# Query and key products term by term, and the token banks filled by transposes, in a fused block of channel attention, token attention and experts

## The chip, the cores and the metric

The kernel runs on one core of a Trainium2 chip. The metric is the device time of one execution in microseconds, median of several. A core has TensorE (PE, matrix products; its weight loads are shown apart as PEld), VectorE (DVE), ScalarE (ACT), GpSimd (POOL) and SyncE (SP, which here only issues DMA). Each takes its own instructions in order and waits on semaphores for the others.

## The reference

```python
# layer 0, per image (16 images, 192 channels, 32 x 32 points)
xn = (x - mu) * rsqrt(var + EPS) * ln_g + ln_b
Q, K, V = (dwconv3x3(per_head_1x1(xn)) for each of q, k, v)       # 8 heads of 24
attn = softmax(einsum('bhnc,bhnd->bhcd', K, Q) / alpha)           # channels x channels
x = einsum('bcij,oc->boij', V attn, w_f) + b_f + xn
# layer 1, on tokens t [16, 1024, 192]
t = t + causal_attention(_ln_t(t))        # 6 heads of 32, output projected twice
t = t + experts(_ln_t(t))                 # 4 experts of 768, top 2, gelu
```

All is float32; the gates choose the experts from the normed tokens.

## The kernel before

A first part runs over the 16 images, one after the other; a second runs over 67 blocks of 512 routed rows and does the experts. Only the first part is touched. Each engine has one program, written out by hand in order; nothing reorders it but the weight loads of PE. In an image of 1024 tokens in 8 chunks of 128:

1. The convolutions give query, key and value channels; channel attention is computed and folded with w_f into mixing matrices `mix`.
2. **Token banks.** For each chunk k one PSUM bank (`token_bank(k)` = k modulo 6) collects the tokens of the chunk, 192 columns of channels and 4 of gates: `input_and_first_heads` brings in the normed image `xn` (two halves of 96 channels, as products with an identity), the gate columns, and the first heads; `last_heads` the others. DVE takes each bank (`channel_mixed`, line 1045, signal `y_sb`), takes statistics (`first_stats`), and POOL raises the variance to the power -1/2 (`token_rstd`, line 716).
3. **Norm.** DVE writes the normed chunks (`normed`, line 1021), four at a time, PE transposes them (`norm_transposes`, line 1714) into two banks. ACT copies these rounded (`T0`, `T1`; line 1458, signal `T_hi`), DVE forms the remainders (`low_channels`, lines 1029 and 1032; `T2` and the lower part of `T1`; signal `T_lo`).
4. **Query and key products** (`queries_keys`, line 1731). There are six groups n, each a weight block f for a half nh of the tokens, in the order of `QK_ORDER`; each is five products of 512 columns (the entries of `qkv`: two with T0, one with T2, two with T1) into bank n modulo 4. ACT copies the group (`QKh`, line 1551), DVE forms its remainder (`low_qk`, line 1038, signal `qk_lo`). Groups 0 to 2 and the values of two chunks come ahead of the norm transposes of the second half, groups 3 to 5 behind them.
5. **Values** (`values_of_tokens`, line 1739): five products of 192 columns for each chunk.
6. SP and POOL copy QKh and QKl into stacks `KS`, `QS` by DMA, in three waves of tokens; from them come the scores (line 1770), exponentials, block transposes (line 1782) and the weighted values of the causal attention. POOL copies the inverse sums wide (`inverse_wide`, lines 728 and 729) for PE's transposes at line 1822.

DVE's order in steps 2 to 4 matters: chunks 0 to 4, `normed` of the first half, chunks 5 and 6, `low_channels` of the first half, chunk 7, `low_qk(0)`, `normed` of the second half, `low_qk(1)` and `(2)`, `low_channels` of the second half, `low_qk(3)` to `(5)`. Between these steps stands part of the previous image's routing; its rows are scattered by POOL (`send`, line 780, two scatters for each chunk).

The waits of `queries_keys`: a group n below 4 waits for `y_sb`, since its bank was a token bank: n = 0 for chunk 6's bank, n = 1 and above for chunk 7's; n = 4 and 5 wait for `low_qk` of groups 0 and 1.

Of the kernel before, what the change touches and what calls it, by code (L numbers as in the profile page):

```python
# [15 lines left out]
P = 128  # L16
# [3 lines left out]
def hybrid_block_kernel(nc, x, ln_g, ln_b, conv_w, conv_bias_row, conv_taps, conv_bias, alpha_rows, w_f_t, b_f,  # L20
                        w_qkv_a, w_qkv_b, w_proj, w_proj_t, b_proj, gate_w_a, gate_w_b, gate_b, w1_a, w1_b, b1_t,
                        w2, b2, out):
    B, C, SH, SW = x.shape
    N = SH * SW
    NC = N // P
    HALF = C // 2
# [13 lines left out]
    E = gate_w_a.shape[1]  # L40
# [3 lines left out]
    CE = C + E  # L44
    QC = N // BANK
    TPC = BANK // P
# [24 lines left out]
    with ExitStack() as ctx:  # L71
# [183 lines left out]
        def bank(b, n=1):  # L255
            return ps[:, b * BANK:(b + n) * BANK]
# [200 lines left out]
        NORM_BANK = (6, 4)  # L457

        def value_bank(k):
            return (6, 7, 4, 5)[k % 4]  # L460

        QK_ORDER = [(0, 0), (1, 0), (2, 0), (0, 1), (1, 1), (2, 1)]
        NQ = len(QK_ORDER)
# [186 lines left out]
        def _(pool):  # L650
# [138 lines left out]
            for i in range(B):  # L789
                unpad_image(pool, i)  # L790
                if i:
                    send(i - 1, 0, 3)
                token_rstd(i, 0)
                if i:
                    send(i - 1, 3, 5)
                token_rstd(i, 1)
                if i:
                    send(i - 1, 5, 6)
                pool.wait_ge(qk_hi, NQ * i + PAIR_GROUPS)
                for j in range(2):  # L800
                    load_queries(g, 0, j, 0, QKh)
                    load_queries(g, 0, j, 2, QKh)
                pool.wait_ge(qk_lo, NQ * i + PAIR_GROUPS)
                for j in range(2):
                    load_queries(g, 0, j, 1, QKl)
                if i:
                    send(i - 1, 6, NC)
                output_bias(i, 0)
                for qc in range(NC):
                    inverse_wide(i, qc)  # L810
                    if qc == 0:
                        output_bias(i, 1)
                    if qc == 2 and i + 1 < B:
                        image_rstd(pool, i + 1)
                    if qc == TPC:
                        token_rstd2(i, 0)
                    if i + 1 == B:
                        split_behind(qc)
                token_rstd2(i, 1)
# [603 lines left out]
        def _(act):  # L1423
# [31 lines left out]
            def high_channels(i, j):  # L1455
                for n, dst in enumerate((T0, T1)):
                    act.wait_ge(lnT_ps, 4 * i + 2 * j + n + 1)
                    a.activation(dst[:, BANK * j:BANK * (j + 1)], bank(NORM_BANK[j] + n), ACT.Copy).then_inc(T_hi, 1)
# [67 lines left out]
            for i in range(B):  # L1526
                conv_qk(i, 0)
                if i:
                    gate_exp(i - 1)
                conv_out(i, 2)  # L1530
                conv_qk(i, 1)
                conv_out(i, 3)
                channel_exp(i, 0)
                conv_out(i, 4)
                conv_qk(i, 2)
                mixing(i, 0)
                conv_out(i, 5)
                conv_qk(i, 3)
                channel_exp(i, 1)
                mixing(i, 1)  # L1540
                high_channels(i, 0)
                for n in range(NQ):
                    if n == QK_FIRST:
                        for k in range(2):
                            values_out(i, k)
                        high_channels(i, 1)
                    f, nh = QK_ORDER[n]
                    if i == 0 and n == 0:
                        act.wait_ge(w_ld["zero"], 16)
                    act.wait_ge(qk_ps, NQ * i + n + 1)  # L1550
                    a.activation(QKh[:, f, BANK * nh:BANK * (nh + 1)], bank(n % 4), ACT.Copy).then_inc(qk_hi, 1)
                for k in range(2, NC):
                    values_out(i, k)
                for n, (qc, h) in enumerate(SOFT):
                    exponentials(i, n)
                    if n:
                        blocks_out(i, n - 1)
                    if qc and h == 2:
                        norms_out(i, qc - 1)
                blocks_out(i, NU - 1)  # L1560
                if i + 1 < B:
                    for r in range(2):
                        conv_out(i + 1, r)
                norms_out(i, NC - 1)
# [44 lines left out]
        def _(pe):  # L1609
# [82 lines left out]
            def input_and_first_heads(i, k):  # L1692

                o = bank(token_bank(k))
                t.matmul(o[:, 0:HALF], xn[:, 0, P * k:P * (k + 1)], ident[0:HALF, 0:HALF],
                         start=True, stop=False, skip_group_check=True)
                t.matmul(o[:, C:CE], xn[:, 0, P * k:P * (k + 1)], gcol[:, :], start=False, stop=False,
                         skip_group_check=True)
                t.matmul(o[:, HALF:CE], xn[:, 1, P * k:P * (k + 1)], ident_g[:, :], start=False, stop=False,
                         skip_group_check=True)  # L1700
                t.matmul(o[:, 0:CE], vp[:, 0, P * k:P * (k + 1)], mix[:, 0, :], start=False, stop=False,
                         skip_group_check=True)

# [13 lines left out]

            qkv = ((T0, wqa_hi), (T0, wqa_lo), (T2, wqa_hi), (T1, wqb_hi), (T1, wqb_lo))

            def queries_keys(i, n):  # L1720
                f, nh = QK_ORDER[n]
                if n >= 4:
                    pe.wait_ge(qk_lo, NQ * i + n - 3)
                if n < 4:
                    pe.wait_ge(y_sb, NC * i + min(NC - 1 + n, NC))
                for m, (act_part, w_part) in enumerate(qkv):
                    if f == 0 and m in (0, 3):
                        pe.wait_ge(T_hi, 4 * i + 2 * nh + 1 + m // 3)
                    if f == 0 and m in (2, 3):
                        pe.wait_ge(T_lo, 4 * i + 2 * nh + m - 1)  # L1730
                    last = t.matmul(bank(n % 4), w_part[:, P * f:P * (f + 1)],
                                    act_part[:, BANK * nh:BANK * (nh + 1)], start=m == 0, stop=m == 4)
                last.then_inc(qk_ps, 1)

            def values_of_tokens(i, k):
                if k >= 4:
                    pe.wait_ge(v_done, NC * i + k - 3)
                for m, (act_part, w_part) in enumerate(qkv):
                    last = t.matmul(bank(value_bank(k))[:, 0:C], act_part[:, P * k:P * (k + 1)],
                                    w_part[:, 2 * C:3 * C], start=m == 0, stop=m == 4)  # L1740
                last.then_inc(v_ps, 1)
# [105 lines left out]
            for i in range(B):  # L1847
# [32 lines left out]
                    input_and_first_heads(i, k)  # L1880
                    last_heads(i, k)
                norm_transposes(i, 0)
                for n in range(QK_FIRST):
                    queries_keys(i, n)
                for k in range(2):
                    values_of_tokens(i, k)
                norm_transposes(i, 1)
                for n in range(QK_FIRST, NQ):
                    queries_keys(i, n)
                for k in range(2, NC):  # L1890
                    values_of_tokens(i, k)
                if not i:
                    pe.wait_ge(setup_pool, 8)
# [179 lines left out]
```

## Time and profile before

| | |
|---|---|
| median of 3 runs (lowest, highest) | 3336.41 us (3331.54, 3340.59) |
| profiled execution, its own time | 3334.18 us |
| its span in the trace | 3332.3 us |
| PE busy | 3067.4 us, 92% |
| DVE busy | 2202.3 us, 66% |
| ACT busy | 1871.5 us, 56% |
| POOL busy | 874.5 us, 26% |

The images take the time to about 2210 us, the experts the rest. Times in the trace are from the start of the span; all numbers below are in that clock. A row of the timeline has start, duration, engine, line, operation and the idle time ahead of it with what ended it. Durations of products overlap, so the cost of one in a row is the distance of the starts.

### The profile page before, as it was taken

To read this page: it belongs to the slowest core of one execution; us is meant where nothing else is said; L and a number is where in the kernel's file an instruction comes from. 1 tells how busy PE (TensorE), PEld (TensorE's weight loads), DVE (VectorE), ACT (ScalarE), POOL (GpSimd) and SP (SyncE) were. 2 spreads that over 40 slices of the span, in tenths; PEclk is the share of its full clock that TensorE was granted. 3 is DMA by queue.
4 is the path that set the end of the run, shared out by engine and by line. 5 is a ranking of instruction groups with operands and counts; after the bars stand their busy time and mean duration, and the time that the engine had idled before them with its cause. 6 is when DMAs were issued, how large, how long until landed. Compare 5 with 4: busy or idle time off the path is not lost. (4 is left out here: it accounts for less than half of the span.)

```text
span 3332.3 us, 72396 instructions
## 1 busy us (share of the span) xinstructions
PE 3067.4 (92%) x26642; PEld 2344.2 (70%) x26642; DVE 2202.3 (66%) x5619; ACT 1871.5 (56%) x3996; POOL 874.5 (26%) x1142
## 2 busy tenths in 40 slices
PE   4999999999999999999999999958999999999995
PEld 1666667666666676666766766637888888888884
DVE  3777677677776776777767767664555655655653
ACT  0647456465474664654746647535555555555553
POOL 2121313303223133132230331450223223223222
PEclk9999999999999999999999999979999999999997
DMA  7546445454364454544644546515667767667673
GB/s 177 142 114 178 115 124 148 124 150 126 113 184 116 122 149 122 153 118 120 173 125 115 148 123 154 156 47 159 195 206 213 221 208 220 210 205 228 206 212 120
DMA packets 256516, 519.82 MB, mean 156 GB/s; under 512 B 70919, under 2 KB 161991, under 8 KB 246521
## 3 DMA queue, kind: packets, MB, share of 16 engines
q1 hardware_dynamic: 222878, 453.58, 48.6%
q0 software_dynamic: 29184, 59.81, 6.0%
q8 instruction: 217, 3.56, 0.4%
q10 hardware_dynamic: 4107, 1.81, 0.3%
q14 instruction: 130, 1.06, 0.1%
HBM read 242.82 MB, written 117.71 MB: 108 GB/s over the span
## 5 line engine op out<-in xcount | busy, mean ns | idle before, releaser
L1051 DVE TENSOR_REDUCE minus_max<-ps 128x1 f32<-128x128 f32 (+7 forms) x768 | 571.6, 750 | 243.7 <-PE ps L1772 232.3
L1469 ACT ACTIVATE p_sb<-ps,minus_max 128x128 f32<-128x128 f32 (+7 forms) x768 | 569.3, 741 | 41.3 <-DVE minus_max L1051 37.8
L1782 PE MATMUL ps<-ident,p_sb 128*128 128x128 f32 x3456 | 530.6, 279 | 44.2 <-ACT p_sb L1469 18.4
L1356 DVE TENSOR_TENSOR g_lo<-g,g_hi 128x512 fp32r<-128x512 f32 x402 | 282.8, 704 | 369.3 <-ACT g_hi L1593 369.3
L1592 ACT ACTIVATE g<-ps,bcur 128x512 f32<-128x512 f32 x402 | 276.6, 688 | 429.2 <-PE ps L1967 429.2
L1483 ACT ACTIVATE PT<-ps 128x512 f32<-128x512 f32 (+3 forms) x768 | 396.7, 517 | 132.7 <-PE ps L1782 123.5
L1782 PEld LDWEIGHTS ps<-ident,p_sb 128*128 128x128 f32 x3456 | 370.0, 141 | 99.4 <-ACT p_sb L1469 37.5
L1983 PE MATMUL ps<-w_all,g_hi 128*128 x1608 | 434.6, 351 | 0.0
L1770 PE MATMUL ps<-KS,QS 96*128 96x512 f32 (+3 forms) x1152 | 393.6, 401 | 21.4 <-ACT p_sb L1469 17.9
L1647 PE MATMUL ps<-ring,wconv 125*32 125x512 f32 (+1 forms) x3072 | 358.4, 606 | 15.0 <-DMA ring<-padded_scratch 15.0
L780 POOL DMA_INDIRECT routed_rows<-xhat,slot x256 | 253.3, 989 | 358.2 <-issue 358.2
L846 POOL DMA_INDIRECT got<-expert_rows,slot x256 | 257.6, 1006 | 333.6 <-issue 270.7
L728 POOL COPY inverse_wide<-inverse_sums 128x192 f32<-128x192 f32 x128 | 44.2, 345 | 1040.3 <-DVE inverse_sums L1072 1040.3
L1988 PE MATMUL ps<-w_all,g_lo 128*128 x1608 | 293.1, 264 | 0.0
L1988 PEld LDWEIGHTS ps<-w_all,g_lo 128*128 128x128 f32 x1608 | 289.4, 188 | 2.0
L1983 PEld LDWEIGHTS ps<-w_all,g_hi 128*128 128x128 f32 x1608 | 263.8, 191 | 22.8
L1593 ACT ACTIVATE g_hi<-ps,bcur 128x512 fp32r<-128x512 f32 x402 | 273.5, 680 | 0.0
L1967 PE MATMUL ps<-X_hi,cur 128*128 128x512 f32 x804 | 264.9, 411 | 7.5 <-ACT g_hi L1593 5.6
L1967 PE MATMUL ps<-X,cur 128*128 128x512 f32 x804 | 250.0, 392 | 0.0
L1770 PEld LDWEIGHTS ps<-KS,QS 96*128 96x128 f32 x1152 | 196.9, 195 | 69.4 <-ACT p_sb L1469 42.4
L1647 PEld LDWEIGHTS ps<-ring,wconv 125*32 125x32 f32 (+1 forms) x3072 | 94.2, 111 | 207.5 <-issue 192.7
L1064 DVE COPY PT<-ps 128x128 f32<-128x128 f32 (+3 forms) x384 | 184.9, 482 | 67.6 <-PE ps L1782 67.5
(276 smaller groups left out, 5442.5 us busy)
## 6 DMA issues: line engine op xcount, KB each, us to landing
ring<-padded_scratch SPq DMA_DIRECT2D x576, 204.0 KB
cur<-w_all SPq DMA_DIRECT2D x67, 1536.0 KB, 7.1
routed_rows<-zero_rows SPq DMA_DIRECT2D x67, 384.0 KB, 5.0
xgt<-routed_rows SPq DMA_DIRECT2D x67, 384.0 KB, 4.6
expert_rows<-y_rows SPq DMA_DIRECT2D x67, 384.0 KB, 3.0
padded_scratch<-xpad SPq DMA_DIRECT2D x32, 435.0 KB, 3.6
x_sb<-x SPq DMA_DIRECT2D x16, 768.0 KB, 5.5
KS<-QKh SPq DMA_DIRECT2D x128, 96.0 KB
```

The source lines that it names most:

```text
L1051: v.tensor_reduce(nmx[:, qc, h:h + 1], score_place(n), AX, ALU.max, negate=True).then_inc(mx_sb, 1)
L1356: v.tensor_tensor(g_lo[:, n % 2, :], g32[:, n % 2, :], g_hi[:, n % 2, :].bitcast(F32), ALU.subtract).then_inc(lo_sb, 1)
L1469: a.activation(p_sb[n % NP][:, 0:P * (qc + 1)], score_place(n), ACT.Exp, bias=nmx[:, qc, h:h + 1], accum_out=ls[:, qc, h:h + 1]).then_inc( ...
L1483: a.activation(PT[h][:, k0:k0 + nb, :], bank(pass_bank(t))[:, 0:P * nb].rearrange("p (k q) -> p k q", q=P), ACT.Copy).then_inc(PT_act, 1)
L1592: a.activation(g32[:, n % 2, :], bank(n % 2), ACT.Gelu, bias=b1)
L1593: a.activation(g_hi[:, n % 2, :], bank(n % 2), ACT.Gelu, bias=b1).then_inc(gelu_sb, 1)
L1647: last = t.matmul(bank(2 * (r % 2) + nh)[W * j:W * (j + 1), :], wconv[s][0:KROWS[s], h, c0:c0 + W], rhs, start=s == 0, stop=s == 1, skip_g ...
L1770: t.matmul(o[:, k0:k0 + keys], QS[0:96, qc // TPC, h, P * (qc % TPC):P * (qc % TPC + 1)], KS[0:96, h, k0:k0 + keys], start=True, stop=k0 + ...
L1782: last = t.transpose(bank(pass_bank(piece))[:, P * k:P * (k + 1)], p_sb[n % NP][:, P * (k0 + k):P * (k0 + k + 1)], ident[:, :])
L1967: last = t.matmul(bank(n % 2), w[:, W1L * part + P * j:W1L * part + P * (j + 1)], act_part[:, :], start=m == 0, stop=m == 4)
L1983: t.matmul(bank(acc_bank(r, tt))[:, 0:2 * C], g_hi[:, n % 2, P * tt:P * (tt + 1)], w2j, start=j == 0, stop=False, skip_group_check=True)
L1988: last = t.matmul(bank(acc_bank(r, tt))[:, 0:C], g_lo[:, n % 2, P * tt:P * (tt + 1)], w2j[:, 0:C], start=False, stop=j == J - 1, skip_grou ...
```

## The change

It has four parts. In the token banks each half of `xn` enters as a transpose (a product in the transposing mode) of 96 columns instead of a product with the identity, and the gate columns of each half come in a product of four columns of their own. In `queries_keys` the three groups of a half are taken together, term by term: the two products with T0 of all three groups, then T2 of all three, then T1 of all three. The values of chunks 2 and 3 move ahead of the second three groups, on PE and on ACT, with other banks. POOL's scatters of chunk 5 move behind its query loads.

```diff
         def value_bank(k):
-            return (6, 7, 4, 5)[k % 4]
+            return (6, 7, 6, 7, 4, 5, 6, 7)[k]
...
                 token_rstd(i, 1)
-                if i:
-                    send(i - 1, 5, 6)
                 pool.wait_ge(qk_hi, NQ * i + PAIR_GROUPS)
...
                 if i:
-                    send(i - 1, 6, NC)
+                    send(i - 1, 5, NC)
...
                         high_channels(i, 1)
+                        for k in range(2, TPC):
+                            values_out(i, k)
...
-                t.matmul(o[:, 0:HALF], xn[:, 0, P * k:P * (k + 1)], ident[0:HALF, 0:HALF],
-                         start=True, stop=False, skip_group_check=True)
-                t.matmul(o[:, C:CE], xn[:, 0, P * k:P * (k + 1)], gcol[:, :], start=False, stop=False,
-                         skip_group_check=True)
-                t.matmul(o[:, HALF:CE], xn[:, 1, P * k:P * (k + 1)], ident_g[:, :], start=False, stop=False,
-                         skip_group_check=True)
+                for h in range(2):
+                    t.matmul(o[:, HALF * h:HALF * (h + 1)], xn[:, h, P * k:P * (k + 1)], ident[0:HALF, 0:HALF],
+                             start=h == 0, stop=False, is_transpose=True, skip_group_check=True)
+                    t.matmul(o[:, C:CE], xn[:, h, P * k:P * (k + 1)],
+                             (gcol[:, :], ident_g[:, HALF:HALF + E])[h], start=False, stop=False, skip_group_check=True)
...
+            def queries_keys(i, nh):
+                group = range(QK_FIRST * nh, QK_FIRST * (nh + 1))
+
+                def term(n, m):
+                    f = QK_ORDER[n][0]
+                    act_part, w_part = qkv[m]
+                    return t.matmul(bank(n % 4), w_part[:, P * f:P * (f + 1)],
                                     act_part[:, BANK * nh:BANK * (nh + 1)], start=m == 0, stop=m == 4)
+                pe.wait_ge(T_hi, 4 * i + 2 * nh + 1)
+                for n in group:
+                    if n >= 4:
+                        pe.wait_ge(qk_lo, NQ * i + n - 3)
+                    else:
+                        pe.wait_ge(y_sb, NC * i + min(NC - 1 + n, NC))
+                    term(n, 0)
+                    term(n, 1)
+                pe.wait_ge(T_lo, 4 * i + 2 * nh + 1)
+                for n in group:
+                    term(n, 2)
+                pe.wait_ge(T_hi, 4 * i + 2 * nh + 2)
+                pe.wait_ge(T_lo, 4 * i + 2 * nh + 2)
+                for n in group:
+                    term(n, 3)
+                    term(n, 4).then_inc(qk_ps, 1)
 
             def values_of_tokens(i, k):
-                if k >= 4:
+                if k in (2, 3):
+                    pe.wait_ge(v_done, NC * i + k - 1)
+                if k in (6, 7):
                     pe.wait_ge(v_done, NC * i + k - 3)
...
-                for n in range(QK_FIRST):
-                    queries_keys(i, n)
+                queries_keys(i, 0)
                 for k in range(2):
                     values_of_tokens(i, k)
                 norm_transposes(i, 1)
-                for n in range(QK_FIRST, NQ):
-                    queries_keys(i, n)
-                for k in range(2, NC):
+                for k in range(2, TPC):
+                    values_of_tokens(i, k)
+                queries_keys(i, 1)
+                for k in range(TPC, NC):
                     values_of_tokens(i, k)
```

On PE, one chunk of the token banks before and after, behind the channel products of line 1674 (line 1695 is the identity product, 1696 in the new kernel the transpose):

```order
L1674 MATMUL ps<-qkt 64x64 x16
L1695 MATMUL ps<-ident,xn 128x96
L1697 MATMUL ps<-gate_cols,xn 128x4
L1699 MATMUL ps<-ident_gate,xn 128x100
L1701 MATMUL ps<-mix,vp 128x196
```

```order
L1674 MATMUL ps<-qkt 64x64 x16
L1696 MATMUL ps<-ident,xn 128x96
L1698 MATMUL ps<-gate_cols,xn 128x4
L1696 MATMUL ps<-ident,xn 128x96
L1698 MATMUL ps<-ident_gate,xn 128x4
L1700 MATMUL ps<-mix,vp 128x196
```

The product of 100 columns is split into a transpose of 96 and a product of 4.

On PE, the first half's groups, behind the norm transposes of image 0; before, the first two groups (T_hi is T0, T_lo is T2, T_128 is T1):

```order
L1731 MATMUL ps<-T_hi,wqkv_a_lo 128x512
L1731 MATMUL ps<-T_lo,wqkv_a_hi 128x512
L1731 MATMUL ps<-T_128,wqkv_b_hi 128x512
L1731 MATMUL ps<-T_128,wqkv_b_lo 128x512
L1731 MATMUL ps<-T_hi,wqkv_a_hi 128x512
L1731 MATMUL ps<-T_hi,wqkv_a_lo 128x512
L1731 MATMUL ps<-T_lo,wqkv_a_hi 128x512
```

```order
L1725 MATMUL ps<-T_hi,wqkv_a_hi 128x512
L1725 MATMUL ps<-T_hi,wqkv_a_lo 128x512
L1725 MATMUL ps<-T_hi,wqkv_a_hi 128x512
L1725 MATMUL ps<-T_hi,wqkv_a_lo 128x512
L1725 MATMUL ps<-T_hi,wqkv_a_hi 128x512
L1725 MATMUL ps<-T_hi,wqkv_a_lo 128x512
L1725 MATMUL ps<-T_lo,wqkv_a_hi 128x512 x3
L1725 MATMUL ps<-T_128,wqkv_b_hi 128x512
L1725 MATMUL ps<-T_128,wqkv_b_lo 128x512
```

Six products now stand ahead of the first that reads the remainder T_lo, and the first group is finished by the eleventh of fifteen instead of by the fifth.

On POOL, between the two roots of the variances and the first wide copy of the inverse sums, before and after (each DMA of line 780 is a scatter of rows, line 357 loads queries):

```order
L716 TENSOR_TENSOR rstd<-rstd,minus_half 128x4
L780 DMA routed_rows<-xhat_0_137,slot 34304x192 x2
L357 DMA QS<-QKh 32x3x256 x4
L357 DMA QS<-QKl 32x3x256 x2
L780 DMA routed_rows<-xhat_0_137,slot 34304x192 x4
L786 TENSOR_TENSOR t_sb<-t_sb,bproj_bc 128x784
```

```order
L716 TENSOR_TENSOR rstd<-rstd,minus_half 128x4
L357 DMA QS<-QKh 32x3x256 x4
L357 DMA QS<-QKl 32x3x256 x2
L780 DMA routed_rows<-xhat_0_137,slot 34304x192 x6
L786 TENSOR_TENSOR t_sb<-t_sb,bproj_bc 128x784
```

Two scatters have moved behind the query loads, so six stand in a row ahead of the bias addition at line 786.

## Rows read from the trace of the kernel before

**Rows 1.** The list of waits of PE: engine line waited for: us, times, longest

```profile
PE ps L1822 <- POOL inverse_wide L729: 14.4, 32, 3.3
```

**Rows 2.** Timeline of PE, eighth image, one chunk of the token banks

```profile
1038.37 0.36 PE L1695 MATMUL ps<-ident,xn 96*128 96x96 f32 x2
1038.56 0.31 PE L1697 MATMUL ps<-gate_cols,xn 96*128 96x4 f32 x2
1038.73 0.45 PE L1699 MATMUL ps<-ident_gate,xn 96*128 96x100 f32 x2
1039.01 0.52 PE L1701 MATMUL ps<-mix,vp 128*128 128x196 f32 x2
1039.37 0.83 PE L1705 MATMUL ps<-mix,vp 128*128 128x196 f32 x4
```

**Rows 3.** Weight loads: line 1695 (ns least/median/most), line 1782 (count, us busy, mean ns)

```profile
L1695 PEld LDWEIGHTS ps<-ident,xn x256: 186/191/193, 90.5 to 2111.7; 96*128 96x128 f32 x128
...
L1782 PEld LDWEIGHTS ps<-ident,p_sb 128*128 128x128 f32 x3456 | 370.0, 141 | 99.4 <-ACT p_sb L1469 37.5
```

**Rows 4.** Timeline of DVE, eighth image

```profile
1037.67 0.63 DVE L1045 TENSOR_TENSOR t_sb<-ps,bf_bc 128x196 f32<-128x196 f32 x2 [0.22 <-PE ps L1705]
...
1046.70 0.36 DVE L1045 TENSOR_TENSOR t_sb<-ps,bf_bc 128x196 f32<-128x196 f32 x1
...
1048.18 0.69 DVE L1038 TENSOR_TENSOR QKl<-ps,QKh 128x512 fp32r<-128x512 f32 x1 [0.30 <-ACT QKh L1551]
1049.04 1.35 DVE L1021 TENSOR_SCALAR xhat<-t_sb,tmv,rstd 128x192 f32<-128x192 f32 x4 [0.17 <-POOL rstd L716]
```

**Rows 5.** Timeline of PE, second image (first row), then the eighth

```profile
247.06 0.44 PE L1714 MATMUL ps<-ident,xhat 128*128 128x128 f32 x2 [0.17 <-DVE xhat L1021]
...
1043.49 1.09 PE L1714 MATMUL ps<-ident,xhat 128*128 128x128 f32 x8 [0.62 <-DVE xhat L1021]
1044.92 0.47 PE L1731 MATMUL ps<-T_hi,wqkv_a_hi 128*128 128x512 f32 x1 [0.34 <-DVE t_sb L1045]
...
1046.81 0.47 PE L1731 MATMUL ps<-T,wqkv_b_hi 128*128 128x512 f32 x1 [0.32 <-DVE T L1032]
1047.12 0.40 PE L1731 MATMUL ps<-T,wqkv_b_lo 128*128 128x512 f32 x1
...
1049.65 0.25 PE L1739 MATMUL ps<-wqkv_a_hi,T_hi 128*128 128x192 f32 x1
...
1050.75 1.04 PE L1714 MATMUL ps<-ident,xhat 128*128 128x128 f32 x8
...
1059.75 0.24 PE L1770 MATMUL ps<-KS,QS 96*128 96x128 f32 x1
```

**Rows 6.** Timeline of ACT, eighth image

```profile
1047.55 0.60 ACT L1551 ACTIVATE QKh<-ps 128x512 fp32r<-128x512 f32 x1 [2.29 <-PE ps L1731]
```

**Rows 7.** Timeline of POOL, sixth image (first row), then the eighth

```profile
791.34 0.96 POOL L780 DMA_INDIRECT routed_rows<-xhat,slot  x1 [1.50 <-issue]
...
1055.25 1.03 POOL L780 DMA_INDIRECT routed_rows<-xhat,slot  x1 [0.30 <-issue]
...
1060.13 1.86 POOL L786 TENSOR_TENSOR t_sb<-t_sb,bproj_bc 128x784 f32<-128x784 f32 x1
1065.24 0.34 POOL L728 COPY inverse_wide<-inverse_sums 128x192 f32<-128x192 f32 x1 [3.25 <-DVE inverse_sums L1072]
```

**Rows 8.** Stretches of 2 us: length, busy PE, PEld, DVE, ACT, POOL, clock, DMA

```profile
104.00:106.00 2.00, 0.58 (x5) 0.58 (x6) 1.81 (x7) 0.00 (x0) 0.01 (x1) 1.00 0.00 0
...
108.00:110.00 2.00, 1.98 (x4) 1.31 (x5) 1.71 (x6) 0.00 (x0) 0.11 (x1) 0.50 0.00 0
...
1044.00:1046.00 2.00, 1.28 (x9) 0.64 (x7) 1.90 (x8) 1.09 (x2) 1.39 (x3) 1.00 0.15 51
```

**Rows 9.** Timeline of PE, first image, query and key products

```profile
109.31 0.63 PE L1731 MATMUL ps<-T,wqkv_b_lo 128*128 128x512 f32 x1
109.74 0.63 PE L1731 MATMUL ps<-T_hi,wqkv_a_hi 128*128 128x512 f32 x1
```

More of the change, by code:

```diff
@@ L1718, in _ @@
             qkv = ((T0, wqa_hi), (T0, wqa_lo), (T2, wqa_hi), (T1, wqb_hi), (T1, wqb_lo))
[L1720 to L1731, printed above, removed]
-                                    act_part[:, BANK * nh:BANK * (nh + 1)], start=m == 0, stop=m == 4)
-                last.then_inc(qk_ps, 1)
+            def queries_keys(i, nh):
[4 more added lines that the diff above has]
+                    return t.matmul(bank(n % 4), w_part[:, P * f:P * (f + 1)],
+                                    act_part[:, BANK * nh:BANK * (nh + 1)], start=m == 0, stop=m == 4)
+                pe.wait_ge(T_hi, 4 * i + 2 * nh + 1)
[14 more added lines that the diff above has]
+                    term(n, 4).then_inc(qk_ps, 1)
             def values_of_tokens(i, k):
-                if k >= 4:
+                if k in (2, 3):
+                    pe.wait_ge(v_done, NC * i + k - 1)
+                if k in (6, 7):
                     pe.wait_ge(v_done, NC * i + k - 3)
@@ L1887, in _ @@
                 norm_transposes(i, 1)
-                for n in range(QK_FIRST, NQ):
-                    queries_keys(i, n)
-                for k in range(2, NC):
+                for k in range(2, TPC):
+                    values_of_tokens(i, k)
+                queries_keys(i, 1)
+                for k in range(TPC, NC):
                     values_of_tokens(i, k)
```

## The prediction

> **What bounds the kernel now.** I read the page first. TensorE (PE) is the busiest engine and the chain that ended last runs mostly over it, so its idle time counts, and only that. The list of waits says where PE idles and for whom; one entry on which a term rests is 14.4 us at the transposes of the inverse sums, for POOL's inverse_wide [rows 1], spread over all images. Then I read one image closely, the eighth, in the timelines of PE, DVE, ACT and POOL from 1029.9 us on. Images 2 to 15 (counted from 0) repeat it within 0.1 us. Image 1 differs in one place, named below. Image 0 has no routing beside it and I give it nothing.
>
> In this image the row to look at is the DVE's. It waits 0.22 us for PE at the first channel_mixed, and from there to the last T_lo remainder it waits for PE nowhere [rows 4]. It computes four normed chunks, on which PE's transposes wait 0.62 us, then chunks 5 and 6, then two remainders (low_channels), and only then channel_mixed of chunk 7, from 1046.70 to 1047.06 [rows 4, 5]. That order is not touched by the change.
>
> **Token banks, part by part.** A chunk takes 0.19 + 0.17 + 0.28 + 0.36 = 1.00 us on PE before the next group starts [rows 2]. Each float32 product is two instructions (the 128 chunks of line 1695 have 256 records), a transpose is one (the blocks of line 1782 have 3456). So a chunk has eight instructions before, and eight after: transpose, 2, transpose, 2, 2 of the mixing. The count does not fall; what may fall is the price of one. The products of four columns cost 0.17 / 2 = 0.085 us each by their starts, and the 96 columns about 0.1 each, so it is the loading of weights and not the streaming that sets them. A transpose's load takes 141 ns where a product's takes 191 [rows 3], 0.05 less. Of the two new transposes one follows a mixing product, under whose streaming its load is hidden before and after; the other can give 0.05 us. Bounds: 0 if loads are paced by something else, 0.11 (a whole pass of 96 columns) above. I take 0.05, by the difference of the load rows.
>
> Who profits? Five chunks stand ahead of the first last_heads, so y_ps comes 0.25 us earlier. DVE could use 0.22 us of it, plus 0.05 because its channel logits, which PE feeds behind chunk 0, come earlier too. So DVE moves ahead by 0.25 us; all other savings of PE (3 more chunks) only lengthen its wait for xhat from 0.62 to about 0.77 us. 0.25 us x 14 images + 0.05 for image 1, where DVE is busy without a gap, is **-3.6 us** (bounds 0 and -4.9).
>
> **Query and key products.** The reordering puts six products (two terms of three groups) ahead of the wait for T_lo. But the second group of a half writes bank 1, which channel_mixed of chunk 7 must have read, and so waits for y_sb 8. DVE gives that after both remainders. So PE does two products (the first at 1044.92, the second 0.31 us later) and stops; the wait for T_lo is not covered but replaced by a longer one. Before, PE went on without a gap from 1046.81 [rows 5]. It started 0.11 us after DVE had gone on to its next instruction (1046.70). After the change the releasing row is that next one, of 0.36 us; with the same lag PE starts at 1046.70 + 0.36 + 0.04 + 0.11 = 1047.2, with 13 products left. By the rows the first spacing is 0.31 us and the rest (1049.65 - 1047.12) / 11 = 0.23 [rows 5]: the values of tokens start at 1047.2 + 0.31 + 12 x 0.227, about 1050.2, where they started at 1049.65. **+0.6 us.**
>
> More follows behind it. Group 0 is now finished by the ninth of these 13, not by the second after the wait. The ninth starts at 1049.1; ACT copies 0.43 us later (before: 1047.12 to 1047.55 [rows 5, 6]), and DVE's low_qk(0), which started 0.63 us after ACT [rows 4], runs from 1050.17 to 1050.86. Behind low_qk(0) in DVE's queue stand the four normed chunks of the second half. They started at 1049.04; now at 1050.85, and end at 1052.2. PE's second set of transposes waits for them: 1052.25 instead of 1050.75 [rows 5], with 0.9 us idle ahead. **+1.5 us there.** In image 1 POOL's late rstd held them back anyway (247.06 is 21.14 us after that image's first product at 225.92, against 20.85 in the eighth [rows 5]), so there it is +1.2.
>
> Then the gain. From the second transposes to the first score PE took 1059.75 - 1050.75 = 9.0 us [rows 5]. It holds 0.92 us of transposes, 15 products x 0.227 = 3.41 and 30 of the values x 0.111 = 3.34, together 7.6; the other 1.4 us are waits for T_hi, T_lo and T. With the values of chunks 2 and 3 (1.1 us) between, ACT and DVE finish T of the second half (about 1055.0) before its first use at about 1055.7, six products into the group. All 1.4 us go. Net at the first score: 1.5 - 1.4 = +0.1 us in 14 images and about -0.3 in image 1, in sum **+1.1 us** (bounds -2 and +5: 0.2 and 0.3 us an image for the lags). What is late next? low_qk of the last group: PE's last three groups now end 0.45 us apart, ACT and DVE need 0.6 to 0.69 each, and DVE ends at about 1059.4; the scores wait for it and start at 1059.85. It is just hidden, by the four chunks of values that are left (2.2 us). It would cost up to 0.5 us an image if the lags are longer.
>
> **POOL.** Two scatters of rows move behind the query loads. The queries are no longer late; nothing waited for that. The other end of the queue: six scatters, 1.28 us apart, from 1055.25 end at 1062.9 instead of 1060.1, the bias addition (1.86 us) ends at 1064.8, and inverse_wide is asked for at 1065.24 [rows 7]. Hidden by 0.4 us. But in 6 of 15 images one of these scatters waits 1.2 to 1.7 us more (1.50 at 791.34 [rows 7]). There inverse_wide comes 0.7 to 1.2 us late and PE, which has almost no slack at the norm transposes, stands. ACT's exponentials are the tight resource in these first chunks, so I count half: 6 x 0.9 / 2 = **+2.7 us** (bounds 0 and 15 x 0.9 = 13).
>
> **The clock.** In image 0 PE's granted clock fell to 0.50 just when it started these products: it had been busy 0.58 of 2 us shortly before [rows 8]. Products are then 0.43 us apart (109.31 to 109.74 [rows 9]) instead of 0.23. In the other images PE was busy 1.28 of 2 us and the clock stayed at 1.00 [rows 8]. The change makes this stretch emptier: between about 1045.6 and 1047.2 PE now does nothing, so 2 us that held 1.3 us of work hold 0.3 to 0.5. A fall costs (0.43 - 0.23) x 8 products ahead of the end of group 0 = 1.6 us at the second transposes, and as much at the scores. No row says how often it will happen. I count 3 falls of 15, nearer to none, because 15 images with 1.28 busy never fell and one with 0.58 did: **+4.5 us** (bounds 0 and 15 x 1.5 = 22).
>
> **Sum.** -3.6 + 1.1 + 2.7 + 4.5 = +4.7 us on the profiled execution's 3334.18, which is 2.2 us under the median of 3336.41. That gives 3338.9 for such an execution and 3341.1 for the median; I predict **3341 us**.
>
> **Rivals.** *The clock falls in most images.* For it speaks that the new idle stretch, 1.7 us behind only two products, is emptier than the one of image 0; against it that the 0.62 us ahead of the transposes and 0.34 us behind them, with two more waits close by [rows 5], never made it fall in 15 images. It would give 15 x 1.5 = 22 instead of 4.5: about 3359. It decides from some eight falls on. The Trainium skill, page "TensorE: Matmul & The Clock Gate", section "Part 4: PE-mode transpose", says that transposes do not count as busy for the clock as products do; by it the eight norm transposes and the new transposes in the banks are no help, and this rival is likelier. The trace agrees in part: in image 0 nearly all that PE did in the emptier stretch was transposes. Chance 0.15.
>
> *POOL becomes late in all images*, since six scatters now run while SP's key and query loads fill the DMA engines: 13 us instead of 2.7, about 3351. For it: extra waits appear only in that stretch. Against it: nine images had none. Chance 0.12.
>
> *The wait is covered as the order intends*: if y_sb 8 were there before T_lo, the second transposes would start no later than now, and the 1.4 us of waits in the second half would go for nothing: 1.5 x 14 = 21 less than in the forecast, about 3320. DVE's order speaks against it. Chance 0.05.
>
> *Forecast*, with parts as above: 0.68.
>
> **How the numbers follow.** A measurement can tell about 0.3% here, 10 us. The forecast's chance splits 0.02 faster, 0.52 within, 0.14 slower (when its two positive terms come out at twice their size); the first rival is slower; the second 0.10 slower and 0.02 within; the third faster. Faster 0.07, same 0.54, slower 0.39. The range reaches from 3330 (both positive terms zero, the bank term in full: 3336.4 - 4.9 - 2 = 3329.5) to 3359, where the first rival lies; beyond are the third rival and the worst of both slow ones.
>
> **What would show it.** Right: in a middle image PE idles about 1.5 us at its third product of the first half with DVE's t_sb as releaser, about 0.9 us at the second transposes behind DVE's xhat, and nowhere in the second half; DVE's wait at the first channel_mixed is gone; bank products have the same count of records. Wrong: idle time still at T_lo or T, the first score more than 0.3 us from 29.8 us after the image's first product without a fall of the clock, a chunk under 0.89 us, or L728 waiting for POOL's own queue in most images.

## The result, and the profile after

The changed kernel takes 3357.11 us (median of 6 runs, 3352.58 to 3360.75); before took 3336.36 us in its 6 runs beside it. The ratio is 1.0063 (95% interval 1.005 to 1.0076): 0.63% slower, about 21 us. The forecast was 3341 with a range of 3330 to 3359; the time lies inside the range, near its upper end.

The profiled execution took 3356.89 us. First its page (span, busy time of each engine, the scatters' line), then the list of waits of PE (us in total, times, longest):

```profile
span 3355.0 us, 72396 instructions
...
PE 3067.1 (91%) x26642; PEld 2350.3 (70%) x26642; DVE 2193.9 (65%) x5619; ACT 1864.6 (56%) x3996; POOL 877.2 (26%) x1142
...
L780 POOL DMA_INDIRECT routed_rows<-xhat,slot x256 | 251.7, 983 | 402.8 <-issue 402.8
```

```profile
PE ps L1713 <- DVE xhat L1019: 35.3, 31, 2.6
...
PE ps L1725 <- DVE t_sb L1043: 22.5, 26, 1.5
...
PE ps L1834 <- POOL inverse_wide L729: 15.5, 31, 4.5
```

PE has as many instructions as before and is busy as long (3067.1 us against 3067.4), so on balance the 22.7 us that the span gained are idle time. The balance hides two changes of the busy time: it is 7.7 us less in the token banks, and 6.1 us more between the first norm transposes and the first score, where products ran at a lower clock (below). Line 1834, where I had put POOL's cost, grew from 14.4 [rows 1] to 15.5 us only. The waits grew at the norm transposes (line 1713, before 10.9 us) and at the query/key products for t_sb (line 1725, before 5.5 us); those for T and T_lo (before 9.8 and 5.6 us) are no longer in the list.

Then one image, the third (number 2, counted from 0), whose first bank product is at 363.7 us. PE:

```profile
377.04 1.09 PE L1713 MATMUL ps<-ident,xhat 128*128 128x128 f32 x8 [0.86 <-DVE xhat L1019]
378.52 0.47 PE L1725 MATMUL ps<-T_hi,wqkv_a_hi 128*128 128x512 f32 x1 [0.39 <-DVE t_sb L1043]
...
380.67 0.50 PE L1725 MATMUL ps<-T_hi,wqkv_a_hi 128*128 128x512 f32 x1 [1.45 <-DVE t_sb L1043]
...
385.57 1.09 PE L1713 MATMUL ps<-ident,xhat 128*128 128x128 f32 x8 [0.57 <-DVE xhat L1019]
...
393.25 0.25 PE L1782 MATMUL ps<-KS,QS 96*128 96x128 f32 x1
```

DVE in the same image:

```profile
371.24 0.63 DVE L1043 TENSOR_TENSOR t_sb<-ps,bf_bc 128x196 f32<-128x196 f32 x2
...
378.81 0.69 DVE L1027 TENSOR_TENSOR T_lo<-ps,T_hi 128x512 fp32r<-128x512 f32 x1
379.53 0.69 DVE L1030 TENSOR_TENSOR T<-ps,T 64x512 fp32r<-64x512 f32 x1
380.25 0.36 DVE L1043 TENSOR_TENSOR t_sb<-ps,bf_bc 128x196 f32<-128x196 f32 x1
...
384.28 1.24 DVE L1019 TENSOR_SCALAR xhat<-t_sb,tmv,rstd 128x192 f32<-128x192 f32 x4
```

This is the picture that the prediction drew. DVE starts `channel_mixed` without a gap (before 0.22 us [rows 4]). PE stands 1.45 us at its third product until both remainders and chunk 7's bank are done, waits again at the second transposes, and reaches the first score 29.6 us after the image's first product. But of all images only this one and the last look quite so. In images 4, 5, 10, 12 and 14 the first transposes come 0.3 to 0.4 us later and the rest is the same. In the seven others from number 3 on they come 1.0 to 1.7 us later. The eighth (number 7, first product at 1036.1) shows what these seven have. POOL first:

```profile
1036.52 1.07 POOL L780 DMA_INDIRECT routed_rows<-xhat,slot  x1 [15.85 <-issue]
1041.73 0.96 POOL L780 DMA_INDIRECT routed_rows<-xhat,slot  x1 [4.14 <-issue]
...
1047.78 1.04 POOL L716 TENSOR_TENSOR rstd<-rstd,minus_half 128x4 f32<-128x4 f32 x1
...
1053.29 0.96 POOL L780 DMA_INDIRECT routed_rows<-xhat,slot  x1 [1.95 <-issue]
```

The same place in the kernel before:

```profile
1032.81 0.96 POOL L780 DMA_INDIRECT routed_rows<-xhat,slot  x1 [0.30 <-issue]
1035.72 0.96 POOL L780 DMA_INDIRECT routed_rows<-xhat,slot  x1 [1.95 <-issue]
...
1038.25 0.96 POOL L780 DMA_INDIRECT routed_rows<-xhat,slot  x1 [0.30 <-issue]
1040.80 1.04 POOL L716 TENSOR_TENSOR rstd<-rstd,minus_half 128x4 f32<-128x4 f32 x1 [1.59 <-DVE rstd L1012]
```

POOL sends six scatters ahead of the first `token_rstd`. Before, the fourth of them stalls for 1.95 us (up to 2.8 in other images), and here POOL still waits 1.59 us for DVE ahead of the rstd. After the change the second one stalls, for 4.14 us; the six end one behind the other, and the rstd comes at once behind the last, 11.7 us after the image's first product instead of 10.9. Then PE in the changed kernel, and two stretches of 2 us of the ninth image (length, busy PE, PEld, DVE, ACT, POOL, clock, DMA):

```profile
1050.47 1.63 PE L1713 MATMUL ps<-ident,xhat 128*128 128x128 f32 x8 [1.83 <-DVE xhat L1019]
1051.95 0.78 PE L1725 MATMUL ps<-T_hi,wqkv_a_hi 128*128 128x512 f32 x1
1052.52 0.63 PE L1725 MATMUL ps<-T_hi,wqkv_a_lo 128*128 128x512 f32 x1
1054.10 0.79 PE L1725 MATMUL ps<-T_hi,wqkv_a_hi 128*128 128x512 f32 x1 [0.95 <-DVE t_sb L1043]
```

```profile
1186.00:1188.00 2.00, 1.19 (x8) 1.05 (x8) 1.93 (x7) 0.49 (x1) 1.39 (x2) 0.85 0.14 49
1188.00:1190.00 2.00, 1.46 (x4) 0.50 (x2) 1.93 (x5) 0.70 (x2) 0.35 (x1) 0.50 0.16 53
```

The first transposes of the eighth image wait 1.83 us and those of the ninth 2.42 us, and the granted clock goes to its lower level, 1.2 GHz, just there (0.50 in the second stretch).

All 16 images by the timelines (us from the image's first bank product; "falls" counts images whose query/key stretch has products at the lower clock; "T to score" is from the first norm transposes to the first score, as undisturbed images, those without a fall, show it; the first two columns leave out image 0):

| kernel | rstd(0) on POOL | first transposes | T to score | falls |
|---|---|---|---|---|
| before | 10.9 | 13.57 | 16.26 | 1 |
| changed | 10.7 to 12.4 | 13.38 to 15.12 | 16.21 | 9 |

The nine images with a fall are the seven with the late rstd and images 0 and 1; the five that are late by 0.3 to 0.4 us have none. A trace counts the falls of one execution, but the mean granted clock of the whole span agrees with it in the others: 0.975 to 0.977 in the six runs of the change, 0.981 to 0.985 in the 29 runs of before that stand beside experiments 1 to 4.

The 22.7 us part as follows, summed over the images. First transposes: +9.2 (-2.7 for the banks, +12 for the late rstd in images 3 to 14). From there to the first score: +10.9 (falls +11.5, the rest -0.6). Behind it +0.5, ahead of image 0 -1.0, behind image 15 the remaining 3.1, which is not traced further.

### The profile page after: what moved, and what is told of

Read it like the earlier page. It is cut to its first block and busy times, and to the rows that moved or that the text cites. A ratio compares the mean times of both kernels' runs of the same rounds, so it can differ in the third digit from the quotient of the medians.

```text
span 3355.0 us, 72396 instructions
## 1 busy us (share of the span) xinstructions
PE 3067.1 (91%) x26642; PEld 2350.3 (70%) x26642; DVE 2193.9 (65%) x5619; ACT 1864.6 (56%) x3996; POOL 877.2 (26%) x1142
```

## Experiments

"Restored order" below is the changed kernel with before's order of the scatters.

**1. The change without its POOL part.**

```diff
+                if i:
+                    send(i - 1, 5, 6)
                 pool.wait_ge(qk_hi, NQ * i + PAIR_GROUPS)
...
-                    send(i - 1, 5, NC)
+                    send(i - 1, 6, NC)
```

> The changed kernel with POOL's order as it was: the two scatters of chunk 5 ahead of the query loads again; everything else as changed. Theory A (POOL's new order makes the first root of the variances late in 9 images, 12.1 us in sum at the first norm transposes, and the longer idle time there lets the clock fall in more images, 11.7 us in sum): the idle time ahead of the first transposes goes back to about 0.86 us in every image, 12 us come back from there and a part of the falls, so 3336 to 3344 us. Theory B (the order of the query and key products is what costs, and POOL is late only as a consequence of it): POOL's root stays late in those images and the time stays within 4 us of 3357.

3342.42 us, ratio 1.0015 (1.0004 to 1.0026). The rstd comes at 10.7 and the first transposes at 13.39 in every image from the third on. Falls in 5 images. 15 us of the 21 are gone. So most of the loss goes with the POOL order, as theory A has it. Image 0 is one of the five, and it has a fall in before too.

**2. The POOL part alone**, in the kernel before (the reverse of that diff).

> The kernel before with POOL's new order alone: the two scatters of chunk 5 behind the query loads. Theory A: the stall of POOL's second scatter (3.3 to 4.9 us in the changed kernel) appears here too, the first norm transposes come up to 1.6 us later in about nine images: 3345 to 3352 us, more if the clock falls. Theory B: no stall moves, since it comes from the products' order: 3334 to 3339 us.

3357.83 us, ratio 1.0059 (1.0046 to 1.0072): all of the loss, without any product moved, and more than the 3345 to 3352 us expected. The two parts (1.0015 and 1.0059) add to 1.0074, against 1.0063 for both together; the difference is within the intervals. POOL in the eighth image:

```profile
1039.43 1.07 POOL L780 DMA_INDIRECT routed_rows<-xhat,slot  x1 [15.87 <-issue]
1044.45 0.96 POOL L780 DMA_INDIRECT routed_rows<-xhat,slot  x1 [3.95 <-issue]
...
1050.49 1.04 POOL L716 TENSOR_TENSOR rstd<-rstd,minus_half 128x4 f32<-128x4 f32 x1
```

The stall is at the second scatter again, the first transposes come at 13.7 to 15.1, later by 10.9 us in sum. Here the clock falls in few images (4, 8, a little in 6), so the falls are not a consequence of the late rstd alone; from the transposes to the score 6.7 us are added in sum, in undisturbed images 0.3 each. Of the 26 us that this profiled execution takes more than before's, another 8.4 lie behind the first scores, 5.9 of them behind that of image 15 (experiment 1 has 5.6 there too). They are not traced, so 17.6 of the 26 us are shown to go with the late rstd.

**3. The token banks alone**, in the kernel before (the part of the diff in `input_and_first_heads`).

> The kernel before with the token banks filled by transposes and nothing else. By the trace of the changed kernel the first channel_mixed starts 0.19 us earlier in 14 images: 2.7 us less, about 3334 us. If transposes do not hold the clock up as products do, some images show a fall of the clock in or behind the banks, 1.6 us each: 3336 to 3345 us with falls in the trace.

3335.0 us, ratio 0.9994 (0.9984 to 1.0003). First transposes at 13.38, 0.19 earlier; a fall in image 0 only, as before. The Trainium skill (page "TensorE: Matmul & The Clock Gate", section "Part 4: PE-mode transpose") says that transposes do not count as busy for the clock as products do, and I had held this against the new transposes in the banks. It does not show here: with them the clock fell no oftener, in one image before and after. For the norm transposes no run tells.

**4. Term by term, and the moved values, alone.**

> The kernel before with the query and key products term by term and the values of chunks 2 and 3 ahead of the second half, nothing else (banks and POOL as before). By the spans of images in which the clock did not fall, the stretch from the first norm transposes to the first score costs nothing or gains 0.05 us an image. If the idle time at y_sb 8 alone makes the clock fall: 3 to 8 images with a fall, 1.7 us each, 3341 to 3350 us. If only the late POOL brought the falls: none or one, 3335 to 3338 us.

3342.71 us, ratio 1.0018 (1.0009 to 1.0026). Idle 0.39 and 1.45 us at the first and third product, 0.82 at the second transposes; first score at 30.05 instead of 29.84; falls in 3 images, 0.8 to 1.1 us each. The time is in the range that was expected if the idle time alone brings falls, but a fall costs less than the 1.7 us assumed, and the stretch costs 0.2 us an image where nothing or a small gain was expected.

**5. Chunk 7 ahead of the low halves on DVE**, restored order.

```diff
-                low_channels(i, 0)
                 channel_mixed(i, NC - 1)
+                low_channels(i, 0)
```

> The change with the POOL order of before (as in the run with that order restored), and on DVE the chain of token chunk 7 (channel_mixed) put ahead of the low halves of the normed first half (low_channels(i, 0)), which the third query/key group no longer has to pass. Theory A (the third group waits 1.45 us for chunk 7's y_sb because the low halves stand ahead of it; the row of those halves is about 0.9 us): the third group's first product loses its 1.45 us of idle time, the products after T_lo wait 0.5 to 0.9 us instead, the second transposes do not come later than before; an image is 0.5 to 1.0 us shorter, the whole 8 to 14 us below the restored order's 3342.4, so 3328 to 3335 us, ratio to before 0.9975 to 1.000. Rival (the path of the stretch runs over DVE to the second half's normalized rows, whatever PE waits for): the idle time moves to the second transposes, the first score stays 29.8 us after the image's first product and the time stays 3339 to 3345 us.

3313.47 us, ratio 0.993 (0.9917 to 0.9944): 0.7% faster than before, and 29 us under the restored order where 8 to 14 were expected. PE and DVE in the third image:

```profile
368.36 1.09 PE L1715 MATMUL ps<-ident,xhat 128*128 128x128 f32 x8 [0.86 <-DVE xhat L1021]
369.84 0.47 PE L1727 MATMUL ps<-T_hi,wqkv_a_hi 128*128 128x512 f32 x1 [0.39 <-DVE t_sb L1045]
370.14 0.40 PE L1727 MATMUL ps<-T_hi,wqkv_a_lo 128*128 128x512 f32 x1
370.54 0.50 PE L1727 MATMUL ps<-T_hi,wqkv_a_hi 128*128 128x512 f32 x1
...
371.57 0.85 PE L1727 MATMUL ps<-T_lo,wqkv_a_hi 128*128 128x512 f32 x3
...
375.68 1.09 PE L1715 MATMUL ps<-ident,xhat 128*128 128x128 f32 x8 [0.80 <-DVE xhat L1021]
```

```profile
370.12 0.36 DVE L1045 TENSOR_TENSOR t_sb<-ps,bf_bc 128x196 f32<-128x196 f32 x1
370.40 0.68 DVE L1029 TENSOR_TENSOR T_lo<-ps,T_hi 128x512 fp32r<-128x512 f32 x1
```

The 1.45 us are gone and nothing takes their place; the second transposes wait 0.80 us, as with the restored order alone (0.82). Only the 0.36 us row of chunk 7 went ahead of the remainders, and its statistics stayed behind them, so T_lo comes some 0.3 us later, not 0.9, and six products cover it. From the transposes to the score it takes 15.01 us, instead of 16.26 before and 16.47 with the restored order, and no image falls.

**6. Five unused products where PE stood idle**, restored order.

```diff
                     term(n, 1)
+                    if n == 0:
+                        for m in range(5):
+                            t.matmul(bank(4), wqa_hi[:, 0:P], T0[:, 0:BANK], start=m == 0, stop=m == 4)
```

> The change with the POOL order of before, and five more products (128x512, full speed about 0.22 us each, written to a bank that nobody reads then) on PE after the first query/key group's first two terms, where PE otherwise stands idle for 1.45 us. The output is the same. Theory A (the clock falls in the query/key stretch come with PE's idle time there and cost 0.7 to 1.7 us each; the restored order had five of them): the stretch at full clock is as long as without the filler (within 0.1 us), the falls there go to 0 to 2, and the time comes down by 3 to 7 us from 3342.4, to 3335 to 3340 us. Rival (the falls have no connection with this idle time, or their cost was made up elsewhere): as many falls, 3341 to 3348 us, with the filler's 1.1 us at half speed on top wherever a fall already is.

3333.91 us, ratio to before 0.9994 (0.9983 to 1.0005), 8.5 us under the restored order. From the transposes to the score it takes as long in undisturbed images (16.48 us against 16.47), and a short fall is left in image 0 alone. In the profiled executions this stretch is 5.1 us shorter in sum; the rest of the 8.5 us is not traced. In the sixth image, first with the filler (line 1740), then without it:

```profile
776.08 1.29 PE L1740 MATMUL ps<-T_hi,wqkv_a_hi 128*128 128x512 f32 x5
777.69 0.50 PE L1727 MATMUL ps<-T_hi,wqkv_a_hi 128*128 128x512 f32 x1 [0.32 <-DVE t_sb L1045]
778.03 0.40 PE L1727 MATMUL ps<-T_hi,wqkv_a_lo 128*128 128x512 f32 x1
778.27 0.40 PE L1727 MATMUL ps<-T_hi,wqkv_a_hi 128*128 128x512 f32 x1
```

```profile
781.11 0.71 PE L1727 MATMUL ps<-T_hi,wqkv_a_hi 128*128 128x512 f32 x1 [1.45 <-DVE t_sb L1045]
781.62 0.63 PE L1727 MATMUL ps<-T_hi,wqkv_a_lo 128*128 128x512 f32 x1
782.05 0.63 PE L1727 MATMUL ps<-T_hi,wqkv_a_hi 128*128 128x512 f32 x1
```

The filler takes the idle time but 0.32 us. The products behind it are 0.24 us apart (778.03 to 778.27), without it 0.43 (781.62 to 782.05). More work for PE, on the same path, makes the kernel faster, and what has gone from the stretch is four of its five falls: this is the price of the clock.

**7. The same products in the whole change.**

> The whole change, POOL order included, with the same five unused products in the first query/key group. Theory A (POOL's late rstd makes the first transposes 1.2 to 2.6 us late in 12 images, about 12 us; the rest of the loss, some 11 to 12 us, is clock falls in the stretch that the later start and the two waits bring): the filler takes away only part of the falls, since the idle time ahead of the transposes stays: 3347 to 3354 us against 3357. If the lateness of POOL alone were the loss and the falls cost nothing: 3357 to 3361 us. The first transposes stay at 13.7 to 15.1 us after the image's first product in both.

3347.94 us, ratio to before 1.0045 (1.0028 to 1.0061), 9.2 us under the change. First transposes at 13.4 to 15.0 (late by 9.8 us in sum, 9.2 in the change), falls in 7 images, six of them with 1.9 us or more idle ahead of the first transposes, where the filler does not reach. From the transposes to the score 3.6 us are added in sum to before, 10.9 in the change. As expected by theory A, the filler takes away a part.

**8. The loads behind 14 scatters of an image instead of 10**, whole change.

```diff
                 token_rstd(i, 1)
+                if i:
+                    send(i - 1, 5, 7)
                 pool.wait_ge(qk_hi, NQ * i + PAIR_GROUPS)
...
-                    send(i - 1, 5, NC)
+                    send(i - 1, 7, NC)
```

> The whole change, but POOL sends chunks 5 and 6 (four scatters) ahead of its loads of the queries, and only chunk 7 behind them: 14 of an image's 16 scatters stand ahead of the six loads, where before had 12 and the change has 10. Theory A (POOL's long stall comes at the eighth scatter after the loads of the image before: before 4 scatters of the image and 4 of the next, in the change 6 and 2): with 2 scatters of the image behind the loads the stall moves to the sixth scatter of the next image, is 0.3 to 1.5 us long there since the scatters ahead of it have taken the time, and the first half's rstd comes at 10.7 to 11.2 us; the first transposes start at 13.4 to 13.8 us in every image, and the time falls to 3338 to 3348 us. Rival (any scatter moved from its place behind the second rstd makes the queue late): the stall stays at the second scatter with 3 to 5 us and the time stays at 3355 to 3360 us. A third outcome is that the loads, 2.6 us later on POOL than in before, hold the first scores up by 0.5 to 1 us in each image: then 3350 to 3360 us with the first transposes on time.

3398.37 us, ratio 1.0188 (1.0172 to 1.0205). The stall moved as theory A expected; the time is far outside all three outcomes. POOL in the eighth image, then PE at its first score, then two stretches behind it:

```profile
1054.22 1.07 POOL L780 DMA_INDIRECT routed_rows<-xhat,slot  x1 [15.94 <-issue]
1055.60 0.96 POOL L780 DMA_INDIRECT routed_rows<-xhat,slot  x1 [0.30 <-issue]
...
1063.68 0.96 POOL L780 DMA_INDIRECT routed_rows<-xhat,slot  x1 [3.32 <-issue]
1064.69 1.04 POOL L716 TENSOR_TENSOR rstd<-rstd,minus_half 128x4 f32<-128x4 f32 x1
...
1081.85 1.08 POOL L357 DMA_DIRECT2D QS<-QKl  x2
```

```profile
1085.82 0.30 PE L1784 MATMUL ps<-KS,QS 96*128 96x128 f32 x1 [1.88 <-DMA QS<-QKl]
```

```profile
1085.00:1090.00 5.00, 3.95 (x23) 3.43 (x23) 2.27 (x8) 3.31 (x17) 2.42 (x2) 0.71 0.82 211
1090.00:1095.00 5.00, 4.74 (x31) 2.96 (x30) 2.67 (x9) 3.36 (x14) 2.32 (x3) 0.61 0.93 198
```

The stall sits at the sixth scatter in every image from the third on (1.9 to 3.3 us), in the second at the eighth, as in the other runs; the rstd comes at 10.9 to 11.0 and the first transposes at 13.6. But the loads reach POOL too late: PE waits 26.7 us in all for `QS<-QKl` at the first scores, and behind that wait the clock is at its lower level for some us in nearly every image. I had put 0.5 to 1 us an image on this outcome; with the falls it costs about 3.4.

**9. Chunk 7 first, in the kernel before** (the edit of experiment 5).

> The kernel before, with one edit: DVE does the chain of token chunk 7 ahead of the low halves of the normed first half. Theory A (the step that pays goes with the products' order: term by term, PE needs chunk 7's y_sb before the low halves; a product of five needs the low halves first, at its third term): here the low halves come 0.9 us later and the third product of each image waits 1.2 us instead of 0.34 us, the first score comes 0.5 to 0.9 us later, and the time is 8 to 14 us above before, 3344 to 3350 us, more if the clock falls join. Rival (the DVE order alone is what pays, whatever order the products have): 3315 to 3330 us.

3343.22 us, ratio 1.0013 (1.0 to 1.0025). T_lo is waited for 0.64 us instead of 0.37, the first score comes at 30.1, and the clock falls in two images. The sign is that of the theory, and the size is less than half of it, since again only the 0.36 us row passed. The DVE order pays with products taken term by term; without, it costs 0.25 us an image in the trace, and the interval of the time just reaches 1.

**10. Chunk 7 first, in the whole change.**

> The whole change, POOL order included, and chunk 7's chain ahead of the low halves on DVE. It stands to the run of 3313.5 us with the restored POOL order as the change stands to the restored order, but with the 1.45 us wait gone. Theory A (POOL's late rstd makes the first transposes 12 us late in sum; the falls of the clock need both that idle time and the 1.45 us one): the first transposes come at 13.7 to 15.1 us as in the change, they are followed by 15.0 us to the first score, with falls in 0 to 3 images, and the time is 3323 to 3331 us. Rival (POOL's lateness brings the falls by itself): falls in 6 or more images, 3332 to 3340 us.

3333.14 us, ratio 0.999 (0.9976 to 1.0003). The rival was right: the time and the 8 falls are its own. Without the wait of 1.45 us the transposes' late start is enough: 9 images have 1.8 us or more idle there and 8 of them fall; of the others, with 1.2 us or less, none does. In undisturbed images the stretch takes 15.16 us, as theory A had it.

## Why the prediction was right or wrong

**Token banks** (-3.6 forecast): right in kind, a little large. DVE starts 0.19 us earlier, not 0.25, and 14 images give -2.7. The load of the first transpose of a chunk takes 0.14 us, as forecast, but the second, behind a product of four columns, shows 0.22.

**Query and key products** (+1.1): the mechanism was right at each step: 1.45 us idle for 1.5, 0.57 at the second transposes for 0.9, no wait in the second half. The stretch ends 0.05 us earlier instead of 0.1 later. That last bit belongs to the POOL part: without it (experiments 1 and 4) it is 16.47, +0.2. In the change no scatter runs beside the four normed chunks of the second half, and they take 1.24 us (in before, with one there, 1.35 [rows 4]); with a scatter there in experiment 5, 1.47:

```profile
373.94 1.05 POOL L780 DMA_INDIRECT routed_rows<-xhat,slot  x1 [0.20 <-issue]
...
374.15 1.47 DVE L1021 TENSOR_SCALAR xhat<-t_sb,tmv,rstd 128x192 f32<-128x192 f32 x4
```

**POOL** (+2.7): this step failed. I looked for the cost only behind the moved scatters, at `inverse_wide`, which came no later: from image 1 on its first copy starts 5.5 us behind the image's first score, before and after. (By the rows the last of the six scatters there would end at 1062.7, not at 1062.9; it changes nothing.) The prediction does not mention POOL's stall ahead of the fourth scatter and so takes it as fixed, though it stood in the trace of before (1.95 us, the row at 1035.72 above), with nothing that the profile could name as its end ("issue"). It hangs on what POOL issued before it, and so the moved scatters changed it in the next image. It cost 12 us by itself; the second rival ("POOL late in all images", 3351) had the right engine and nearly the right size, and the wrong place. The Trainium skill (page "DMA: Bandwidth & Descriptors", section "SWDGE vs HWDGE vs iDMA") says that GpSimd itself writes the descriptors of its DMAs into rings that the DMA engines drain. A stall that moves with the number of DMAs issued, as in experiments 2 and 8, would agree with a ring that is full, but no run here shows it.

**The clock** (+4.5): right mechanism, wrong count. I counted three falls of 1.5 us; 9 images fell and the falls cost some 11.5 us. The new idle time alone gave five falls of 0.7 to 1.8 us (experiment 1) and three of 0.8 to 1.1 us (experiment 4), near to what was forecast; with POOL's late rstd ahead of it, idle time at two places close together, most images fell (experiments 1 and 10 show that either place can do it). So the first rival, which I had given 0.15, came in half, driven by the term that I had missed.

**The sum.** -2.7 - 0.6 + 12 + 11.5 = +20 where I had +4.7. With the POOL part undone, experiment 1 took 3342.4 us; the forecast without its POOL term is 3338.4, 4 us less; about 2 of these are the query and key stretch, 0.2 us an image instead of 0.1, and 0.9 the banks. That the time of the change lies inside the range owes something to luck: the range reached to 3359 for the sake of falls in every image (22 us), and what filled it was half of that and a stall of POOL that no term or bound had in the right place.

**What stays open:** what POOL's stall waits for; why experiment 2, with the rstd as late, fell in so few images; its 0.3 us an image in undisturbed ones; and what its profiled execution lost behind the first scores. The version that beats both kernels is that of experiment 5.

## What to carry to other kernels

Products taken term by term hide a late operand only if the other things that the first terms need, here a free bank, are there earlier: put the step that frees the bank ahead of the one that makes the operand, then the order pays. When a DMA is moved on a queue, look at every stall of that queue, in the next iteration too, and treat an unexplained one as something that can move. An idle gap of 1.5 us ahead of matrix work cost 0.7 to 1.8 us more here through the clock, in some iterations and not in others.

## What was not expected of the hardware

POOL's long stall came at the eighth scatter issued after the loads of the queries: before it has 4 scatters of one image behind the loads and stalls at the 4th of the next; the change and experiment 2 have 6 and stall at the 2nd; experiment 8 has 2 and stalls at the 6th; in image 1, with no scatters of an image before it, the stall is at the 8th in all of these kernels. In the change and in experiments 2 and 8 a further one of about 1.95 us follows seven scatters later; before has none there, where POOL has just waited 1.1 us for DVE, though such a pause did not prevent it in experiment 8. The stall takes 3.0 to 4.9 us at the second scatter (1.95 in the last image), 1.9 to 3.1 at the fourth and 1.9 to 3.3 at the sixth. Five unused products of 512 columns in an idle gap saved 8.5 us of 3342. And the DVE row of four normed chunks takes 1.24 or 1.25 us in every kernel where no scatter runs beside it, and 1.25 to 1.50 us, mostly 1.47, where POOL issues one.
